# Mixture-of-experts kernel on one core: rounds 1 to 3 on sorted tokens, in two sets of four blocks

## The reference, cut to what matters

```
xn = layernorm(x)
s  = mixer(xn)        # six 128x128 projections, a scan over time, group norm, gate, output projection
cur = xn
for r in range(4):                                   # four rounds, same experts
    logits = cur @ Wg[r] + bg[r]
    vals, idx = top_k(logits, 2)                     # each token uses 2 of 4 experts
    cw = scatter(softmax(vals), idx)
    y[e] = gelu(cur @ W1[e] + b1[e]) @ W2[e] + b2[e] # 128 -> 512 -> 128
    cur = cur + sum_e cw[e] * y[e]
out = x + s * silu(cur)
```

## Time and profile before

| | us |
|---|---|
| runs (3) | 805.29, 808.48, 808.94, median 808.48 |
| profiled execution, its own time | 802.44 |
| its span, first to last instruction | 800.7 |
| PE, DVE, ACT, POOL busy | 757.6, 623.9, 613.9, 198.8 |

### The profile page before, as it was taken

The page is one execution under the profiler, slowest core; times in us unless marked ns, Lnnn a source line. Parts: engine busy times, 40 slices in busy tenths (PEclk is TensorE's granted clock), DMA queues, the critical chain, the costliest instruction groups (busy, mean ns, idle before and its releaser), DMA issues.

```text
span 800.7 us, 9933 instructions
## 1 busy us (share of the span) xinstructions
PE 757.6 (95%) x3250; PEld 591.2 (74%) x3250; DVE 623.9 (78%) x1035; ACT 613.9 (77%) x858; POOL 198.8 (25%) x223
## 2 busy tenths in 40 slices
PE   8999999999999999999999999999889799758796
PEld 7778777877877777787788778777666677646675
DVE  7999876897896897788788689857699378568456
ACT  7989787887887887788788778778577687466574
POOL 1122111111111111111111111111563016555844
PEclk9999999999999999999999999999979999969898
DMA  8567965332644326533264322644113869949742
GB/s 261 145 120 185 229 154 113 56 97 40 158 107 94 52 40 145 120 92 53 56 143 106 93 39 52 160 100 100 42 41 114 234 197 282 309 130 266 197 128 59
DMA packets 80220, 102.25 MB, mean 128 GB/s; under 512 B 40366, under 2 KB 52138, under 8 KB 76970
## 3 DMA queue, kind: packets, MB, share of 16 engines
q1 hardware_dynamic: 60314, 63.80, 26.3%
q0 software_dynamic: 19440, 37.56, 24.9%
q10 hardware_dynamic: 416, 0.26, 0.1%
HBM read 44.85 MB, written 8.73 MB: 67 GB/s over the span
## 4 chain that ended last, share of the span: by engine, by line
PE 71%; DVE 9%; issue 6%; DMA 4%; ACT 4%; POOL 4%; SPq 1%; POOLq 0%; DVEq 0%; ACTq 0%
PE h_bank L1627 11%; PE h_bank L1631 11%; PE h_bank L1628 11%; PE y_bank L1728 10%; PE y_bank L1716 10%; PE y_bank L1718 10%; PE p_bank L1834 5%; DMA cur<-tmp 4%; DVE g_lo L1294 2%; ACT g L865 2%; ACT g_hi L871 2%; POOL out L744 1%; DVE tmp L1313 1%; POOL cw_b L735 1%; PE r_bank L1766 1%
## 5 line engine op out<-in xcount | busy, mean ns | idle before, releaser
L1294 DVE TENSOR_TENSOR g_lo<-g,g_hi 128x1024 fp32r<-128x1024 f32 x242 | 292.6, 1222 | 142.4 <-ACT g_hi L871 139.6
L865 ACT ACTIVATE g<-h_bank,b_all 128x512 f32<-128x512 f32 x416 | 265.8, 681 | 55.4 <-PE h_bank L1631 54.7
L871 ACT ACTIVATE g_hi<-g 128x1024 fp32r<-128x1024 f32 x242 | 256.8, 1061 | 7.6
L775 POOL DMA_DIRECT2D cur<-tmp x96 | 83.4, 869 | 494.1 <-DVE tmp L1313 330.7
L1627 PE MATMUL h_bank<-cur_hi,w_all 128*128 128x512 f32 x416 | 184.2, 443 | 0.2 <-ACT cur_hi L917 0.2
L1631 PE MATMUL h_bank<-cur_lo,w_all 128*128 128x512 f32 x416 | 163.7, 393 | 0.0
L1628 PE MATMUL h_bank<-cur_hi,w_all 128*128 128x512 f32 x416 | 163.4, 393 | 0.0
L1716 PE MATMUL y_bank<-g_hi,w_all 128*128 128x512 f32 x408 | 157.5, 391 | 0.0
L1718 PE MATMUL y_bank<-g_hi,w_all 128*128 128x512 f32 x392 | 152.6, 389 | 0.0
L1728 PE MATMUL y_bank<-g_lo,w_all 128*128 128x512 f32 x408 | 111.1, 393 | 4.4 <-DVE g_lo L1294 4.4
L1627 PEld LDWEIGHTS h_bank<-cur_hi,w_all 128*128 128x128 f32 x416 | 78.7, 189 | 32.7 <-issue 17.3
(11 more groups left out here) (238 smaller groups left out, 733.8 us busy)
## 6 DMA issues: line engine op xcount, KB each, us to landing
cur<-tmp POOLq DMA_DIRECT2D x113, 256.0 KB
cw_b<-cw_scratch SPq DMA_DIRECT2D x25, 1024.0 KB, 5.8
staged<-w_all SPq DMA_DIRECT2D x34, 512.0 KB
cw_b<-sorted_gates SPq DMA_DIRECT2D x17, 256.0 KB
xn_t<-cur SPq DMA_DIRECT2D x8, 256.0 KB, 5.9
cur<-in_x SPq DMA_DIRECT2D x7, 256.0 KB, 5.3
bench<-sorted_rows SPq DMA_DIRECT2D x6, 266.0 KB, 6.1
xn_scratch<-bench POOLq DMA_DIRECT2D x6, 256.0 KB, 3.1
```

What stands on the lines that cost most here:

```text
L775: pool.dma_start(cur[:, block_of(turn_of(s))], tmp[:, s % SUMS, :], accum_op=ALU.add).then_inc(summed, DMA)
L865: nc.scalar.activation(g[:, gb, ft * BLK:(ft + 1) * BLK], hb[ft][:, :], ACT.Gelu_apprx_tanh, bias=bias_of(s1, ft)).then_inc(gelu_done, 1)
L871: nc.scalar.activation(g_hi[:, gb, h], g[:, gb, h], ACT.Copy).then_inc(g_hi_done, 1)
L1294: nc.vector.tensor_tensor(g_lo[:, gb, h], g[:, gb, h], as_f32(g_hi[:, gb, h]), ALU.subtract).then_inc(g_lo_done, 1)
```

## The change

All eight blocks run rounds 1, 2 and 3 on sorted tokens. They form two sets of four blocks. After the 32 dense steps of round 0 come six lists of 13 items, n = 0 to 5: set n % 2, round n // 2 + 1. List n starts at step 32 + 13 n, and the program has 110 steps. While the items of one set run, the other set is sorted: the sort's places are counted from `after(n)`, the step whose sum is the last that the set needs (15, 31, 44, 57, 70, 83). `load_slots` is the load of PE's registers, now two steps before each list. Every sum is POOL's (`ADDED_BY_DVE_AT` and `add_sum` are gone), and each scatter of rows follows the sum of its step. In rounds 1 to 3 no step is dense, so the spreading of 1 MB of gates for a dense block is gone after round 0, and every step from 32 on stages its weights. Eight blocks are gathered and scattered at the end in place of six; no plain store of the output is left. The mixers start every 10 steps in place of 11. The last block is scattered in two halves after its last product.

```diff
-SORTED = 6
-ITEMS = 2 * SORTED + 5
-TURNS = R * NB - SORTED
-FIRST_ITEM = E * (TURNS - 1)
-LAST_AT = FIRST_ITEM + ITEMS
-STEPS = LAST_AT + E
+SET = 4
+SORTS = 2 * (R - 1)
+LIST = 2 * SET + 5
+ITEMS = SORTS * LIST
+FIRST_ITEM = E * NB
+STEPS = FIRST_ITEM + ITEMS
...
-MIX_AT = (15, 26, 37, 48, 59, 70, 84, 102)
+MIX_AT = tuple(15 + 10 * m for m in range(NB))
...
+def sums_for(n, j):
+    return E * (SET * n + j + 1) if n < 2 else first_step(n - 2) + items_through(j)
+def after(n):
+    return sums_for(n, SET - 1) - 1
...
+SORT_AT = {n: after(n) + 2 for n in range(SORTS)}
+PAIR_AT = {n: after(n) + 3 for n in range(SORTS)}
+PLACE_AT = {n: after(n) + 4 for n in range(SORTS)}
+LIST_AT = {n: after(n) + 6 for n in range(SORTS)}
+ROW_AT = {(n, j): after(n) + 4 + j for n in range(SORTS) for j in range(SET)}
+BACK_END = {(n, j): after(n) + (11, 12, 13)[j // 2 + j % 2] for n in range(SORTS) for j in (0, 1, 3)}
+BACK_MID = {(n, 2): after(n) + 13 for n in range(SORTS)}
+GATES_AT = {(n, h): after(n) + 12 + 2 * h for n in range(SORTS) for h in range(2)}
+SPLIT_SORTED_AT = {(n, j): after(n) + (12, 13, 15, 16)[j] for n in range(SORTS) for j in range(SET)}
+SILU_AT = {(n, j): first_step(n) + items_through(j) + 1 for n in (SORTS - 2, SORTS - 1) for j in range(SET)}
+SILU_AT.update({(SORTS - 2, j): first_step(SORTS - 1) + j - 1 for j in (1, 2, 3)})
+GATHER_AFTER = {(SORTS - 2, 0): 87, (SORTS - 2, 1): 88, (SORTS - 2, 2): 91, (SORTS - 2, 3): 92,
+                (SORTS - 1, 0): 100, (SORTS - 1, 1): 101, (SORTS - 1, 2): 102, (SORTS - 1, 3): 103}
...
# SP's queue, from step 12 on
+            for s in range(E * 3, STEPS):
...
+                elif 0 <= i < ITEMS:
+                    if i + 1 < ITEMS:
+                        stage_w1(i + 1)
+                        load_bias(i + 1)
+                    stage_w2(i)
+                    load_gate(i)
...
+                for n in range(SORTS):
+                    if s == after(n) + 8:
+                        experts.extend(load_list(n, T_EXPERT, "expert"))
+                    elif s == after(n) + 9:
+                        gate_rows.extend(load_list(n, T_GATE, "gate"))
+                    elif s == after(n) + 10:
+                        for j in range(IN_PLACES):
+                            load_rows(n, j)
+                    elif s == after(n) + 12:
+                        load_rows(n, SET - 1)
+                        store_gates(n, 0)
+                    elif s == after(n) + 14:
+                        store_gates(n, 1)
# POOL's queue
-                if s in ADDED_BY_DVE_AT:
-                    continue
...
                 pool.wait_ge(combined, s + 3)
...
+                for n in range(SORTS):
+                    if s == first_step(n):
+                        pool.wait_ge(listed, n + 1)
+                        regs = [pool.alloc_register(f"block{n}_{i}") for i in range(LIST)]
+                        pool.load(regs, tables[0:1, n % 2, T_BLOCK, 0:LIST])
...
+                for n, j in at_step(ROW_AT, s):
+                    scatter_rows(n, j)
+                for n, j in at_step(SILU_AT, s):
+                    pool.wait_ge(row_out, OUT_ORDER.index((n, j)) + 1)
+                    scatter_out(n, j)
+                for n, j in at_step(GATHER_AFTER, s):
+                    gather_sx(n, j)
+            pool.wait_ge(row_out, len(OUT_ORDER))
+            scatter_out(SORTS - 1, SET - 2)
+            for h in range(2):
+                pool.wait_ge(half_done, h + 1)
+                scatter_out(SORTS - 1, SET - 1, range(2 * h, 2 * h + 2))
# PE's queue
+            def load_slots(n):
+
+                regs = [pe.alloc_register(f"slot{n}_{i}") for i in range(LIST)]
+                pe.wait_ge(listed, n + 1)
+                pe.load(regs, tables[0:1, n % 2, T_SLOT, 0:LIST])
...
+                for n in range(SORTS):
+                    if s == first_step(n) - 2:
+                        load_slots(n)
                 if s < STEPS - 2:
                     down(s)
```

More of the change, by code:

```diff
@@ L94 @@
 COUNTS = len(PAIRS) * COLS
 ROW = D + E + 1
-OUT_PLACES, IN_PLACES = 3, 5
-def items_through(j):
-    return min(2 * j + 7, ITEMS)
-def newest_block(i):
-    return min(i // 2, SORTED - 1)
-BANK_JOBS = [("logits", n) for n in range(LAST_TWO)] + [
-    ("sort_logits", 0), ("row", 0), ("row", 1), ("row", 2), ("sort_logits", 1), ("counts", 0), ("row", 3), ("row", 4),
-    ("logits", LAST_TWO), ("row", 5), ("back", 0), ("back", 1), ("gates", 0), ("back", 2), ("back", 3), ("back", 4), ("back", 5),
-    ("gates", 1), ("logits", LAST_TWO + 1)] + [("end", j) for j in range(SORTED)]
@@ new lines @@
+SILU_AT[SORTS - 1, SET - 1] = None
+IDS_AT = {n: after(n) + 15 for n in (SORTS - 2, SORTS - 1)}
+GATHER_AFTER = {(SORTS - 2, 0): 87, (SORTS - 2, 1): 88, (SORTS - 2, 2): 91, (SORTS - 2, 3): 92,
+                (SORTS - 1, 0): 100, (SORTS - 1, 1): 101, (SORTS - 1, 2): 102, (SORTS - 1, 3): 103}
+OUT_ORDER = sorted((key for key, s in SILU_AT.items() if s is not None), key=SILU_AT.get)
+MID, END = 0, 1
+BANK_TIMES = {("logits", n, 0): (s, MID if n == 0 else END) for n, s in LOGITS_AT.items()}
+BANK_TIMES.update({("sort_logits", n, 0): (s, MID) for n, s in SORT_AT.items()})
@@ new lines @@
+BANK_TIMES.update({("counts", n, 0): (s, MID) for n, s in PLACE_AT.items()})
+BANK_TIMES.update({("row", n, j): (s, END) for (n, j), s in ROW_AT.items()})
+BANK_TIMES.update({("back", n, j): (s, END) for (n, j), s in BACK_END.items()})
+BANK_TIMES.update({("back", n, j): (s, MID) for (n, j), s in BACK_MID.items()})
+BANK_TIMES.update({("gates", n, h): (s, MID) for (n, h), s in GATES_AT.items()})
+BANK_TIMES.update({("end", n, j): (s, END) for (n, j), s in SILU_AT.items() if s is not None})
+assert len(set(BANK_TIMES.values())) == len(BANK_TIMES)
@@ L133, with bank_job @@
+BANK_JOBS = sorted(BANK_TIMES, key=BANK_TIMES.get)
+def bank_job(kind, n, j=0):
+    return BANK_JOBS.index((kind, n, j))
+def router_no(kind, n):
+    return [job for job in BANK_JOBS if job[0] in ("logits", "sort_logits")].index((kind, n, 0))
 NORM_GROUPS = [(0, 1), (2, 3), (4, 5, 6, 7)]
@@ L593, in _, with load_list @@
+            def load_list(n, kind, name):
+                regs = [sp.alloc_register(f"{name}{n}_{i}") for i in range(LIST)]
+                sp.wait_ge(listed, n + 1)
+                sp.load(regs, tables[0:1, n % 2, kind, 0:LIST])
+                return [sp.snap(reg, donate=True, min_val=0, max_val=E - 1 if kind == T_EXPERT else ZEROS) for reg in regs]
             copy_block(0)
@@ L676, in _ @@
+            for key in row_stored:
+                sp.wait_ge(row_stored[key], DMA * TPB)
         @block.gpsimd
@@ L779, in _ @@
[L779 to L782 removed]
+                    n, a = item_of(s)
+                    half = cur[:, n % 2 * SET * BLK:(n % 2 + 1) * SET * BLK]
+                    pool.dma_start(half[:, bass.ds(blocks[a] * BLK, BLK)], tmp[:, s % SUMS, :], accum_op=ALU.add).then_inc(summed, DMA)
+                else:
+                    pool.dma_start(cur[:, block_of(s // E)], tmp[:, s % SUMS, :], accum_op=ALU.add).then_inc(summed, DMA)
@@ L841, in take_gates @@
[L841 to L852 removed]
+                act.wait_ge(gates_set, n + 1)
@@ L1202, in token_places @@
+            def token_places(n):
+                job = bank_job("counts", n)
                 before, total = rb[:, 0:COUNTS], rb[:, COUNTS:2 * COUNTS]
+                if n > 0:
+                    for p in range(OUT_PLACES):
+                        dve.wait_ge(row_sent[p], DMA * TPB * len(range(p, SET * n, OUT_PLACES)))
                 dve.wait_ge(r_full, job + 1)
                 dve.wait_ge(consts_made, 3 + 2 * len(PAIRS))
-                link(nc.vector.tensor_tensor_scan(starts, ones[:, :], total, 0.0, ALU.mult, ALU.add))
+                link(nc.vector.tensor_tensor_scan(starts, ones[:, 0:COUNTS], total, 0.0, ALU.mult, ALU.add))
```

895 lines of the change are left out of this document (348 added, 547 removed).

## The result

The changed kernel takes 817.72 us (median of 4 runs, 816.42 to 822.9) against 807.91 of the kernel before: a ratio of 1.0137, with an interval of 1.0094 to 1.018. It is 1.4% slower. The forecast was 796.0, faster; the range of 766 to 838 holds the time, the sign was wrong.

The account below looks back on a forecast made before the run. PE was taken to bound the dense steps and POOL's chain of sums the stretch behind sum 86. Terms 212.5 + 384 + 170 + 22 gave a 788 us span, plus 7.7 to the median: 796, range 766 to 838.

Parts of the forecast that it names:

- steps 0 to 31: First 32 steps: 206.7 us before, less 3.4 for logits, plus 4.5 for sort 0 and 4.7 for register load: 212.5.
- steps 32 to 85: Steps with the other set always being sorted: 92.4 us per 13-step period, 4.15 periods, 384 us.
- combine 85 to the issue of sum 107: Stretch behind sum 86, bound by POOL's sums with scatters and gathers behind them: 164 to 184 us, taken as 170.
- from there to the end: After sum 107: last tanh but one, DVE's finishing, POOL's four scatters, two halves and a landing, about 22 us.
- Sort 0 enters: PE's added work for a sort in steps 0 to 31: logits, count products, eight turns and gates, together 4.5 us.
- Rival B: Rows miss their step because places come late at POOL's first scatter: 10 to 13 us a sort, 829 to 844; chance 0.28.
- The register load: Load of PE's 13 registers for each list, taken as 4.7 us on PE's path, between bounds of 0 and 6.2.
- 4.7, 1 and 3.5 a period: Per 13-step period, us: register load 4.7, sort logits waiting for a sum 1, rows' road and late weights 3.5.
- The four logits that leave: Four logits of dense round 1 leave steps 0 to 31, each priced like a 0.86 us product: 3.4 us less.
- A: PE alone bounds: register loads hide, rows' road and sum before the sort cost nothing; 747, half of it 770; chance 0.14.
- C: DVE's bursts of sorting work hold PE, 8.5 us each: 838 for one a sort, 817 for every second; chance 0.12.
- D: The change doesn't shorten the item work: 13 items are issued whatever the data, so 110 steps are certain; no chance given.

Follow-up runs that it names:

- e1: Changed kernel with each sort's gates and token places moved in DVE's queue between the two low parts of gelu, ahead of the combine; 802.14 us, ratio 0.9946.
- e5: Changed kernel with e1's edit and all sums from 86 to 107 added by DVE in place of POOL's transfers; 773.03 us, ratio 0.9633.
- e11: e5 with each sort's ranking moved in DVE's queue from the middle of step after+3 to behind the combine of step after+2; 770.8 us, ratio 0.9572.
- e2: Changed kernel with each turned row and its scatter one step later, the loading of rows left where it was; 811.15 us, ratio 1.0056.
- e8: Changed kernel with PE's register load written twice per list, but the trace holds no second load, only the changed kernel's instructions; 819.92 us, ratio 1.0193.
- e9: Changed kernel with 24 turns of a constant on PE ahead of the first row of each sort; 808.85 us, ratio 1.0055.
- e12: Changed kernel with only the high part of the weights brought from the fifth staged piece on, the low part left out; 809.65 us, ratio 1.0065.

## Why the prediction was wrong

The sum had four parts up to the end of the span. Each is set beside its stretch; sum 107 was issued at 794.60 in the changed kernel.

| part | forecast, us | trace, us |
|---|---|---|
| steps 0 to 31 | 212.5 | 220.6 |
| steps 32 to 85 | 384 | 395.9 |
| combine 85 to the issue of sum 107 | 170 | 178.1 |
| from there to the end | 22 | 26.5 |
| span | 788 | 821.1 |

In steps 0 to 31 the place wait of list 0 is 3.8 us, its logits wait 2.2 for a sum, and 3.4 us behind the place wait are at half clock. The stretch ends at the start of combine 31, where the 206.7 of the earlier trace rows holds the whole of it, so the miss is 0.7 us more than the table has.

**The step that failed** is "Sort 0 enters: logits 1.1, two count products of about 0.2, eight turns, gates, together 4.5", which then went into the period of 13 steps as "sort 4.5". It counted PE's own work and took DVE's answers to it as hidden. Three instructions of PE in a sort wait for DVE or a sum within a step of each other, and one of them, the first row, can't be on time by the order of the queues, since the counts that DVE has yet to read lie in its bank. That was to be read without a trace of the change: in the kernel before, the count stands in step 90 and the next row at the end of step 91; in the diff `PLACE_AT` and the first `ROW_AT` are the same step, after+4, with DVE's combine, gates and places between them. Rival B had found that the places come late, but hung the price on POOL's scatter, at 10 to 13 us a sort. It is PE's turn that stands, for 3.1 us a sort and some clock, and e1 shows what it is worth: 15.4 us, which is more than the 11.1 (0.0137 of 807.9) by which the changed kernel is slower than the one before, and the larger part of the 21.7 us between forecast and time.

**Terms that were mis-sized.** The register load was 4.7 us a list and is 0.4 at the most by the trace. This error of about 4 us a period runs the other way and hid part of the first in the total: 4.7, 1 and 3.5 a period were forecast, 38 us for steps 32 to 85, and the trace has 30 us of idle time there and the half clock besides, but hardly any of it where the prediction had put it (late sums 2.6, late weights 2.9, rows 0). The four logits that leave were 3.4 us and are 1.0, because the eight matmuls of the batch overlap; the timeline of the kernel before had it, if I had looked at that batch and not at a product:

```profile
184.27 1.06 PE L1766 MATMUL r_bank<-cur,wg_p 128*32 128x512 f32 x8
185.26 1.12 PE L1834 MATMUL p_bank<-desk,pj 128*128 128x512 f32 x2
```

PE's own step was right: outside of sorts and mixers it is 5.44 to 5.45 us in the changed kernel too.

**Behind sum 86** the bound was named rightly. POOL's double groups were forecast at 13.5 us and take 14.1 to 16.0, and 178 us against 170 is within the bounds of 164 to 184. The sign that I had named for being wrong in the kind, POOL waiting for `tmp` behind sum 86, came in part: 16.9 us in three waits, against the 178. That the bound is POOL's sums is shown by e5, not by this sum. What was missed is the clock: it is at half for 13.6 and 17.1 us around the two waits at finished blocks, though PE works only 5.2 and 4.4 us of that. Also the tail: behind sum 107 POOL still has the four scatters of block 1. By the tables they follow step 107; the forecast had them among its twelve single groups ahead of sum 107, where there are eleven, and the 22 us left them out:

```profile
794.60 0.89 POOL L705 DMA_DIRECT2D cur<-tmp  x1 [4.98 <-DVE xn_t L1202]
795.79 1.15 POOL L680 DMA_INDIRECT out<-xn_t,id_i  x1 [0.30 <-issue]
...
812.33 0.98 POOL L680 DMA_INDIRECT out<-cw_b,id_i  x1 [0.30 <-issue]
```

Twelve indirect DMAs lie between 795.8 and 813.3, in place of the eight that were counted.

**The rivals.** A (747 to 770) was far off as a forecast; with both causes gone the kernel comes to its upper edge, 773.0 in e5 and 770.8 in e11. B was wrong in its price, and e2 shows that its road of the rows has less than one step of room. C did not occur: the low part of gelu held PE for 1.3 us in all. That its 817, for a burst in every second sort, is the measured time is luck. Its premise was near, though: DVE was late with its sorting work, but PE stood for that at the row. D held: 110 steps. Of the signs that I had named, the register loads took 1.35 to 3.85 us and "a hole at each" did not come, and the first scatter of each sort stood 3.0 to 3.4 us behind its sum, as the forecast had it.

**The correction to the median** added 6.0 us because the profiled run of before lay that far under its median. The profiled run of after lies 5.2 above its own. So the miss of 33 us in the span is one of 21.7 in the time.

## What to carry to other kernels

When work is added to a full engine's queue, write down for each new instruction what must have answered it or emptied its bank, and in which place of the other engine's queue that answer stands; a wait that the order alone decides is seen in the tables, not in busy shares. In a kernel near its bound a hole of 3 us costs more than 3 us, since the clock behind it falls: moving nine small instructions of DVE ahead was worth 1.9%, and idle turns in the hole alone 0.8%. After an experiment on instructions, count them in its trace: e8's second load was in the source and not in the run. Before work is spread over a queue that is already a chain (here sums that each wait for the landing of the last), ask which engine with room could take the chain away: 22 adds of 0.69 us on DVE removed a stall that moving the gathers and the finishes about had hardly touched.

## What the runs showed of the hardware

- Idle turns of a constant keep PE's clock up and pay: 24 of them in front of six waits of 2.1 to 3.8 us took the clock of a stretch of 532 us from 0.96 to 1.00 and 6.6 us from the time (e9). The shortest of these waits, 2.1 us, was followed by 3.4 us at half clock.
- The eight matmuls of a batch of four logits, 512 columns and 32 output rows each, took 1.0 us together, where the two of a product with 512 columns and 128 rows take 0.86.
- An indirect DMA of 128 rows holds POOL for 0.98 to 2.1 us with 0.3 us between two, twice for longer (2.6 and 3.3 us, changed kernel); the last five of the run still follow each other at 1.29 us, with the transfers nearly idle (DMA share 0.18).
- A register load took 6.16 us on PE's queue in one kernel (17 values) and 1.35 to 3.85 in another (13 values).
- 40 MB less of staged weights, of 174, gave 5.8 us with an uncertainty of 4 (e12), though the DMA share of the changed kernel was 0.81 to 0.83 over 570 us.
